# First attention: TensorE's second ring unit of an even slot ahead of the half weighing instead of behind it

## The reference, cut to what matters

```python
xn = group_norm(x)                       # 8 groups
q, k, v = split(qkv_w @ xn + qkv_b)      # 8 heads of 16 channels, 1024 pixels
attn = softmax((q * scale).T @ (k * scale))
out = proj_w @ (attn @ v) + proj_b + x
```

## Time and profile before

| | |
|---|---|
| median of 3 runs | 5300.02 us (5293.02 to 5305.19) |
| profiled execution | 5304.72 us, span 5302.9 us |
| TensorE busy | 4738.9 us (89%) |
| DVE busy | 3577.1 us (67%) |
| ACT busy | 2996.8 us (57%) |
| granted TensorE clock, mean | 0.959 of full speed |

### The profile page before, as it was taken

How to read it: one execution, slowest core, us unless ns; L and a number is a source line. 1 busy time by engine, 2 the same in 40 slices (tenths; PEclk the granted TensorE clock), 3 DMA queues, 4 the chain that set the end, 5 groups by cost and what they waited for, 6 DMA issues and landing times.

```text
span 5302.9 us, 81731 instructions
## 1 busy us (share of the span) xinstructions
PE 4738.9 (89%) x25633; PEld 2629.4 (50%) x25633; DVE 3577.1 (67%) x7651; ACT 2996.8 (57%) x5516; POOL 1023.8 (19%) x1349
## 2 busy tenths in 40 slices
PE   6999999999999969588888888888999999999999
PEld 1222222222222223367777878777655555555554
DVE  6788888888888636556565655655577667667765
ACT  2666667676676724145555555557655554554552
POOL 2222223222232212023333333333100000000000
PEclk7999999999999989689999999999999999999999
DMA  2622223322233112235454554544211111111112
GB/s 61 166 78 69 73 66 98 84 66 77 66 92 83 49 31 28 68 111 169 135 169 138 154 152 145 162 132 134 64 49 52 45 48 51 47 47 51 49 45 76
DMA packets 396856, 461.35 MB, mean 87 GB/s; under 512 B 86136, under 2 KB 248144, under 8 KB 394320
## 3 DMA queue, kind: packets, MB, share of 16 engines
q1 hardware_dynamic: 362688, 409.11, 26.7%
q0 software_dynamic: 20576, 35.55, 2.4%
q10 hardware_dynamic: 13168, 11.48, 0.8%
HBM read 309.59 MB, written 129.84 MB: 83 GB/s over the span
## 4 chain that ended last, share of the span: by engine, by line
PE 34%; DVE 16%; issue 4%; DVEq 4%; ACT 2%; ACTq 0%; SPq 0%; DMA 0%
PE n_ps_f L2212 4%; PE n_ps_f L2205 4%; PE n_ps_xy L1860 4%; PE n_ps_h L1850 3%; PE n_ps_c L2252 3%; PE n_ps_h L2264 2%; PE n_ps_f L2199 2%; PE n_ps_f L1708 2%; DVEq L2084 1%; PE n_ps_xy L2268 1%; PE n_ps_f L1054 1%; DVE n_stats L1030 1%; PE n_ps_h L2268 1%; DVE n_xln L1042 1%; DVE n_down_weights L2083 1%
## 5 line engine op out<-in xcount | busy, mean ns | idle before, releaser
L664 ACT ACTIVATE a_probs<-ps_b 128x512 f32<-128x512 f32 x2048 | 1111.3, 595 | 558.7 <-PE ps_b L748 535.6
L496 DVE TENSOR_REDUCE a_negmax<-ps_a 128x1 f32<-128x1024 f32 x1024 | 1214.5, 1220 | 242.3 <-PE ps_a L696 213.0
L1663 ACT ACTIVATE n_hidden<-n_ps_h,n_b 128x128 f32<-128x128 f32 x1472 | 419.1, 373 | 346.9 <-PE n_ps_h L1850 346.1
L760 PE MATMUL ps_o<-a_probs,a_v_ones 128*32 128x512 f32 x4096 | 547.6, 607 | 0.5 <-ACT a_probs L664 0.5
L1860 PE MATMUL n_ps_xy<-n_down_weights,n_hidden 128*128 x2944 | 411.9, 284 | 79.2 <-ACT n_xy L1677 73.3
L696 PE MATMUL ps_a<-a_k_stack,a_q_stack 96*128 96x512 bf16 x1408 | 404.0, 394 | 58.5 <-DMA a_k_stack<-split_scratch 27.5
L748 PE MATMUL ps_b<-a_q_stack,a_k_stack 99*128 99x512 bf16 x1408 | 442.3, 386 | 14.8 <-ACT a_probs L664 11.9
L1860 PEld LDWEIGHTS n_ps_xy<-n_down_weights,n_hidden 128*128 128x128 f32 x2944 | 370.7, 196 | 117.3 <-issue 113.2
L2149 ACT ACTIVATE n_down_weights<-n_ps_h 128x512 f32<-128x512 f32 x288 | 172.2, 598 | 427.1 <-PE n_ps_h L2264 319.1
L1850 PE MATMUL n_ps_h<-n_xy,n_up_weights 128*128 128x128 f32 x2944 | 403.2, 281 | 3.2 <-issue 1.5
L1368 POOL DMA_INDIRECT rows_scratch<-n_xln,n_index_out x256 | 257.1, 1004 | 666.8 <-DVE n_index_out L1521 563.2
(11 more groups left out here) (349 smaller groups left out, 8154.3 us busy)
## 6 DMA issues: line engine op xcount, KB each, us to landing
n_up_weights<-in_L_ffn_W_dram SPq DMA_DIRECT2D x368, 256.0 KB
n_up_weights<-score_scratch SPq DMA_DIRECT2D x512, 128.0 KB, 2.9
split_scratch<-a_pieces SPq DMA_DIRECT2D x128, 256.0 KB
rows_scratch<-n_zero SPq DMA_DIRECT2D x16, 1472.0 KB, 9.6
outs_scratch<-n_xy SPq DMA_DIRECT2D x176, 128.0 KB
n_xg<-rows_scratch SPq DMA_DIRECT2D x80, 256.0 KB, 3.4
a_q_stack<-split_scratch SPq DMA_DIRECT2D x66, 256.0 KB, 5.0
a_k_stack<-split_scratch SPq DMA_DIRECT2D x66, 256.0 KB, 5.6
```

The lines of the kernel that those rows point to most:

```text
L496: dve.tensor_reduce(negmax[:, b, t:t + 1], bank, axis=AX.X, op=ALU.max, negate=True).then_inc(ring_read, 1)
L664: act.activation(probs[:, m % PROBS, 512 * k:512 * k + 512], ps_b[:, k, :], ACT.Exp).then_inc(b_exp, 1)
L760: last = pe.matmul(ps_o[32 * j:32 * j + 32, 512 * k:512 * k + 512], v_ones[:, t, J * g + j, :], probs[:, (J * quad + j) % PROBS, 512 * k:5 ...
L1663: last = act.activation(hidden[:, j % 2, f, :], ps_h[j % 2][:, 128 * f:128 * f + 128], ACT.Gelu, bias=b1[:, bass.ds(e, 1), f:f + 1].rearra ...
```

## The change

In an even slot the units behind the first are issued directly behind S, and W follows them. Odd slots, the other engines, the transfers, the buffers and the amounts of work stay as they are; the ring keeps its order of units.

```diff
@@ body, in the program of TensorE
                     n = run(units_of_slot[:1], kind, i, n, table)
                     shifted_scores(i, m)
+                    n = run(units_of_slot[1:], kind, i, n, table)
                     if m >= J:
                         weigh_values(i, m // J - 1, m % J // 2)
                     elif kind != "first":
                         weigh_values(i - 1, G * NT - 1, m % J // 2)
-                    n = run(units_of_slot[1:], kind, i, n, table)
```

## The result

The changed kernel takes 5338.15 us (median of 4 runs, 5333.37 to 5339.44), the kernel before 5299.01 us beside it: a ratio of 1.0072, 95% interval 1.0055 to 1.009. Forecast were 5334 us, 5312 to 5357. The profiled execution has a span of 5335.9 us, 33.0 more than before.

What follows compares the result with a forecast made beforehand. TensorE was taken as nearly dense in the first attention. Stalls of 23.5 us (1.6 per middle image) plus 10 for clock falls made 33.5, so 5338 from the profiled execution, set at 5334 us against the median; range 5312 to 5357.

Steps and rivals of the forecast that it cites:

- slot 2: Sums, waiting for DVE's moments: W is paid behind the wait, but DVE is slower there, so only +0.35 us is left.
- slot 8: Queries, waiting for the normed image: W is paid behind the wait and ACT's exponentials move too, +0.9 us (0.8 to 1.0).
- slots 14, 46: Turns of the maxima: nothing moves in 14, DVE is behind in 46; 0 each, up to 0.2 us.
- slot 28: Scores: bank free 0.3 us into W's time, but the next image's transfer must have landed; 0, bounds -0.3 and +0.4.
- slot 60: Scores, the one gain: bank free, DVE starts its three reductions 1.0 us earlier; -0.6 us an image.
- slots 12, 22 and 38: Keys, values, second sums: the unit waits for a bank DVE is still reducing; +0.35, +0.4 and +0.2 us.
- The rule for a moved unit: W waits for nothing; a unit released d after W's old start stalls TensorE for d, at most 0.99 us, before W.
- The clock: TensorE's clock halves after longer standstills: 8 falls of 14 behind slot 2, none counted for slot 8, 1.3 us each, +10 us.
- the clock holds: Rival: slot 2's standstill is too short to make TensorE's clock fall; 5324 us, chance 0.25.
- Falls in both slots: Rival: TensorE's clock falls behind slot 8 as well as slot 2, nearly every time; about 5357 us, chance 0.14.
- No change: Rival: DVE holds TensorE up behind every stall, so the delays are absorbed; 5304 us, chance 0.06.
- faster: Rival: early readers decide, as in slot 60, and stalls elsewhere vanish behind DVE; 5287 us, chance 0.05.

Runs made afterwards that it cites:

- e2_norm: The kernel before with only slots 2 and 8 (sums and queries) having the second unit ahead of W: ratio 1.0072 to before, median 5336.32 us.
- e3_bank: The kernel before with only slots 12, 22 and 38 (keys, values, second sums) having the second unit ahead of W: ratio 1.0033, median 5315.94 us.
- e4_turns: The kernel before with only slots 14 and 46 (turns of the maxima) having the second unit ahead of W: one run, 5303.94 us.
- e7_query_behind: The kernel before with slot 60's units behind S and W, and slot 8's first query half moved behind S of slot 9: ratio 0.9967, 5284.53 us.
- e5_filler: The changed kernel with one extra overwritten matmul in the waits of slot 2 and slot 8: ratio 1.0042 to the kernel before, median 5318.83 us.

## Why the prediction was right

The time was within 0.1% of the forecast (5338 for 5334). The rise is the stricter test: 39.1 us between the medians for the 33.5 forecast. The order of blocks acts as was argued; within the sum the bank waits and the clock were taken too low, and slot 28 made up for part of it.

| term, us an image | forecast | measured |
|---|---|---|
| slot 2 | +0.35 | +0.40 (e2_norm) |
| slot 8 | +0.9 | +0.87 (e2_norm) |
| slot 12 | +0.35 | +0.46 (e3_bank) |
| slots 14, 46 | 0 | +0.07 (e4_turns) |
| slot 22 | +0.4 | +0.53 (e3_bank) |
| slot 28 | 0 | -0.24 (after, image 13) |
| slot 38 | +0.2 | +0.34 (e3_bank) |
| slot 60 | -0.6 | -0.57 (after) |
| image without a fall | +1.6 | +1.83 (after, image 13) |

- **Stalls, forecast 22.4 us in the 14 middle images, measured some 25.** Six of them (2, 4, 7, 12, 13, 14) have no fall in either trace; they take 1.57 to 2.30 us more than before, 1.80 on the mean. The term mis-sized is slots 12, 22 and 38: 1.33 us an image for 0.95. The waits themselves were read well: 0.45, 0.40 and 0.45 in the profile after, 0.47, 0.4 and 0.42 to 0.5 forecast. But each exchange costs 0.57 to 0.62 at first (e3_bank). In image 13 X starts 0.52, 0.47 and 0.52 us behind the place where W had started, and then holds TensorE longer in front of W than it had in front of S: 1.05 for 0.96 in slot 12 (1.06 in image 7, 921.54 to 922.60), 1.09 for 1.00 in slot 22, 0.31 for 0.25 in slot 38. The rule for a moved unit had no term for that.
- **Slot 8** cost what it should, but the hinge had been put at ACT's exponentials; after the change S of slot 11 (919.09) stands directly behind W of slot 10 (918.09, 1.00 us), TensorE itself. That it is ACT that binds in the old order, e7_query_behind shows.
- **Slot 28** gains 0.24 in the full change (0.32 on the mean of the middle images) and nothing alone. In the full change its unit waits for the transfer in two images and mostly, for 0.3 us, until DVE has read the projection half out of its bank; that the stalls in slots 12 and 22 give the transfer the time is likely, but no run shows it by itself. It had been taken as 0.
- **The clock, forecast +10 us, measured some 12.** The nine stretches cost 15.7 us, read from S of slot 0 to S of slot 13 against images without a fall: 0.81 to 1.65 in the six middle images with one stretch of 3.4 us, 1.40 on the mean, 5.6 in image 8 (13.6 us at half clock; the fall that it had before is added) and 1.6 in image 0. The falls of before had cost some 3.3 us (0.86 in image 8, 1.28 in image 3, some 1.2 in image 0), which the forecast did not take off. So the price of 1.3 was near; the amount was not (37.4 us at half clock, for 8 times 3.4), and the two misses partly cancel. By the Trainium skill's rule (TensorE: Matmul & The Clock Gate, section Terms), the throttled time times the lost share, 37.4 us at half clock would be 18.7 us, an estimate. The trace shows less, 1.4 us for a stretch of 3.4 where the rule gives 1.7.
- **Where the clock fell** was half right. Slot 2 was counted with eight of 14 images and fell in six, with waits of 1.89 us (2.24 in image 8). Slot 8 was counted as nothing, since waits of 1.46 us for the turn mostly passed. That reason held: with 1.43 us it fell in none of eleven images. But in images 0, 8 and 10 the wait had been 0.71 to 0.74 before, not the 0.43 of image 7, and there it is 1.70 to 1.79, and in these three the clock fell. (Image 5, with 1.74, had just had its fall behind slot 2.)
- **Later stages** took 6.1 us less in the profiled execution, with no change in them. Over the runs here that part lies between 3432 and 3440 us, so it is taken for scatter.
- The rivals: *the clock holds* is what e5_filler makes by hand, 5319 for the 5324 given. *Falls in both slots*, nearly every time, did not come: slot 8 fell three times of 15 here and twice in e2_norm, where slot 2 fell in eleven images of 14. *No change* and *faster* are out: the image period rose in 14 of the 16 images by over 1.5 us, and by 0.2 us in the last; image 3 alone is 0.2 shorter, since it had a fall before and none after.

## What to carry to other kernels

On an engine that works in order, a block that waits for nothing is cover: put it ahead of a unit that waits, not behind it, and read the worth of the cover as the end of what the unit waits for less the start of the block (here the unit itself also took 0.06 to 0.10 us longer in front of the block). An earlier unit pays only where its reader is what the engine waits for next, as in slot 60; and a removed wait pays only if no other chain ends at the same place, as e7_query_behind shows. Look at the wait in all images, not in one: the few longer ones were those where the clock fell. Where a standstill grows, count TensorE's clock as a term of its own, at the price that falls in the same kernel show (here 1.4 us for 3.4 us at half clock), take off the falls that are there already, and measure the term apart with work that costs nothing because it fills the wait.

## What the runs showed of the hardware that was not expected

With the same waits (27.7 and about 23 us in all) the clock fell behind slot 2 or 8 in eight images of the changed kernel and in twelve of the run with slots 2 and 8 alone, and stayed at half speed for 3.4, 6.8 or 10.2 us. Behind slot 2 a wait of 1.89 us passed in some images and not in others, in either run. Behind slot 8, both runs together, it fell behind none of the 20 waits of 1.43 us and behind five of the ten of 1.70 to 1.79; the other five stood in images where it had just fallen behind slot 2. Which images it takes behind slot 2 differs between these two nearly equal programs, by 17.0 us at half clock, some 7 us of time at the price above, and nothing read from the trace of before told which. With one matmul of 384 and one of 256 columns put into these waits (e5_filler) it fell behind slot 2 or 8 in no image.
